# The second self attention's values: copied by ScalarE, with their bias added by a one-row product

## What is computed

```python
def _L1_attn_ref(x, W, b):
    ...
    qkv = jnp.einsum('btc,oc->bto', x, W) + b
    q, k, v = jnp.split(qkv, 3, axis=-1)
    ...
    att = jnp.einsum('bhtd,bhsd->bhts', q, k) / math.sqrt(D)
    att = jnp.where(causal, att, -jnp.inf)
    att = jax.nn.softmax(att, axis=-1)
    y = jnp.einsum('bhts,bhsd->bhtd', att, v)
    return y.transpose(0, 2, 1, 3).reshape(B, T, C)

x = x + _L1_attn_ref(_layernorm(x, axis=-1), L1_attn_W, L1_attn_b)
x = x + _L1_ffn_ref(_layernorm(x, axis=-1), ...)
```

## Time and profile before

| | |
|---|---|
| median of the runs | 1271.08 us |
| the profiled execution, its own time | 1269.69 us |
| its span, first to last instruction | 1267.7 us |
| TensorE busy | 1192.1 us, 94% |
| VectorE busy | 811.6 us, 64% |
| ScalarE busy | 642.3 us, 51% |
| GpSimd busy | 558.4 us, 44% |
| mean granted TensorE clock | 0.995 of full |

### The profile page before, as it was taken

The page is one execution under the profiler, slowest core; times in us unless marked ns, Lnnn a source line. Parts: engine busy times, 40 slices in busy tenths (PEclk is TensorE's granted clock), DMA queues, the critical chain, the costliest instruction groups (busy, mean ns, idle before and its releaser), DMA issues.

```text
span 1267.7 us, 30321 instructions
## 1 busy us (share of the span) xinstructions
PE 1192.1 (94%) x9828; PEld 943.1 (74%) x9828; DVE 811.6 (64%) x1773; ACT 642.3 (51%) x1394; POOL 558.4 (44%) x833
## 2 busy tenths in 40 slices
PE   6899999989998878988999999999999999999998
PEld 5677777767775546877776888888888888888886
DVE  4688888867776887658999784444444544444444
ACT  5766666644444887545556434433334334334342
POOL 2244444567775444458886323233232233232332
PEclk9999999999998999999999999999999999999999
DMA  8100000000000000200000234333333433333331
GB/s 284 59 25 17 17 17 8 1 2 2 0 0 19 15 1 26 75 26 2 0 0 1 76 104 133 104 104 111 116 109 110 133 116 105 109 105 116 114 105 63
DMA packets 34041, 80.13 MB, mean 63 GB/s; under 512 B 4416, under 2 KB 12096, under 8 KB 33984
## 3 DMA queue, kind: packets, MB, share of 16 engines
q1 hardware_dynamic: 32800, 78.09, 18.6%
q10 hardware_dynamic: 1184, 1.31, 0.3%
HBM read 77.03 MB, written 2.36 MB: 63 GB/s over the span
## 4 chain that ended last, share of the span: by engine, by line
PE 78%; DVE 8%; issue 5%; POOL 4%; ACT 4%; DMA 0%; DVEq 0%; POOLq 0%; ACTq 0%; SPq 0%
PE ps L2434 10%; PE ps L2435 10%; PE ps L2433 10%; PE ps L2516 5%; PE ps L2515 5%; PE ps L2517 5%; PE ps L444 4%; PE ps L1095 3%; PE ps L459 3%; PE ps L432 3%; PE ps L1086 2%; PE ps L1074 2%; PE ps L1065 2%; PE ps L1102 2%; POOL Sm L1406 2%
## 5 line engine op out<-in xcount | busy, mean ns | idle before, releaser
L2802 POOL TENSOR_TENSOR sw<-sg,wb 128x512 f32<-128x512 f32 x136 | 176.4, 1297 | 386.7 <-ACT sg L2626 352.8
L2705 DVE TENSOR_TENSOR a<-sw,ps 128x512 f32<-128x512 f32 x136 | 93.5, 687 | 224.7 <-POOL sw L2802 224.4
L2631 ACT ACTIVATE ah<-a 128x512 fp32r<-128x512 f32 x136 | 86.0, 632 | 290.8 <-DVE a L2705 268.5
L2433 PE MATMUL ps<-Hh,wh 128*128 128x512 f32 x544 | 215.8, 397 | 0.2 <-DVE a L2705 0.2
L2434 PE MATMUL ps<-Hl,wh 128*128 128x512 f32 x544 | 214.8, 395 | 0.0
L2435 PE MATMUL ps<-Hh,wl 128*128 128x512 f32 x544 | 214.7, 395 | 0.0
L2709 DVE TENSOR_TENSOR al<-a,ah 128x512 fp32r<-128x512 f32 x136 | 95.6, 703 | 62.5 <-ACT ah L2631 59.3
L760 ACT ACTIVATE Pr<-ps,mx 128x256 f32<-128x256 f32 x256 | 104.0, 479 | 60.9 <-DVE mx L629 56.3
L2433 PEld LDWEIGHTS ps<-Hh,wh 128*128 128x128 f32 x544 | 102.1, 188 | 25.5 <-issue 1.3
L2435 PEld LDWEIGHTS ps<-Hh,wl 128*128 128x128 f32 x544 | 102.0, 188 | 25.0
L2434 PEld LDWEIGHTS ps<-Hl,wh 128*128 128x128 f32 x544 | 102.2, 188 | 23.7
(11 more groups left out here) (238 smaller groups left out, 2488.0 us busy)
## 6 DMA issues: line engine op xcount, KB each, us to landing
wb<-token_weights SPq DMA_DIRECT2D x64, 512.0 KB, 3.6
raw<-in_ew SPq DMA_DIRECT2D x66, 384.0 KB, 3.0
cT<-in_ctxT SPq DMA_DIRECT2D x16, 256.0 KB, 2.6
cx<-in_ctxT SPq DMA_DIRECT2D x15, 256.0 KB, 2.6
X<-in_x SPq DMA_DIRECT2D x1, 1536.0 KB, 7.3
wqkv<-in_wqkv SPq DMA_DIRECT2D x2, 768.0 KB, 5.3
raw3g<-in_wg SPq DMA_DIRECT2D x1, 1024.0 KB, 5.0
raw3u<-in_wu SPq DMA_DIRECT2D x1, 1024.0 KB, 7.1
```

Source lines behind the costliest of these rows:

```text
L2433: eng.matmul(ps[:, bank, :], wh[:, u, w], HhT[:, c, cols], start=(c == 0), stop=False)
L2705: eng.tensor_tensor(a[:, tt, :], sw[:, tt, :], ps[:, UB[tt], :], ALU.mult).then_inc(m_a, 1)
L2802: eng.tensor_tensor(sw[:, tt, :], sg[:, tt, :], wb[:, u, tt * UT:(tt + 1) * UT], ALU.mult).then_inc(m_sw, 1)
```

## The change

In layer 5 alone, the bias is added on TensorE, by a third product into the same accumulation: a column of one row of 128 ones against the one row of 256 biases. The four copies on VectorE become four plain copies on ScalarE, in two halves: two after the copy of hT, two after the exponentials of the second half. Layer 2 keeps the old form.

```diff
             for c in range(2):
                 ins = eng.matmul(ps[:, FV, 0:DIM], hT[:, u, c, :], w[:, c, 2 * DIM:3 * DIM],
-                                 start=(c == 0), stop=(c == 1))
+                                 start=(c == 0), stop=(c == 1 and proj))
+            if not proj:
+                ins = eng.matmul(ps[:, FV, 0:DIM], g["ones"][0:1, :], bv[0:1, :], start=False, stop=True)
             ins.then_inc(a_v, 1)
...
# vector, body
-            if front:
+            if front and proj:
                 v_out(i + 1, v)
...
# vector, first
-            v_out(0, 0)
+            if proj:
+                v_out(0, 0)
...
# scalar
+        def v_out(i, u, half):
+            if half == 0:
+                eng.wait_ge(a_v, given(a_v) + i + 1)
+                eng.wait_ge(a_pv, given(a_pv) + 2 * (i - 1))
+            b = half
+            for e in range(2):
+                eng.activation(V[SEQ * e:SEQ * (e + 1), u, :, b, HD * e:HD * (e + 1)],
+                               ps[SEQ * b:SEQ * (b + 1), FV, 0:DIM].rearrange("p (n e d) -> p n e d", e=2, d=HD)[:, :, e, :],
+                               ACT.Copy).then_inc(a_ve, 1)
...
# scalar, body
             if further(i):
                 ln_act(eng, L, i + 2, u, FH)
+            if front and not proj:
+                v_out(i + 1, v, 0)
             if not proj:
                 g["route"]["turned"](eng, i - 3, v)
             if mid:
                 exps(i, 1)
+            if front and not proj:
+                v_out(i + 1, v, 1)
...
# scalar, first
             ln_act(eng, L, 1, 1, FH)
+            if not proj:
+                v_out(0, 0, 0)
+                v_out(0, 0, 1)
```

## The result

The changed kernel takes 1277.7 us in the median of 4 runs (1276.86 to 1279.19), against 1271.03 us (1270.46 to 1272.88) for the kernel before: 1.0054 times as long, with a 95% interval of 1.0035 to 1.0073. That is 6.7 us slower, outside the forecast range of 1268.6 to 1275.0. The profiled execution took 1276.92 us, with a span of 1275.0 us against 1267.7.

A forecast was written before the change was run, and what follows sets the result against it. TensorE, busy 94% of the span, was taken to set the pace once VectorE was relieved. The terms summed to +1.1 us: 1270.8 profiled, 1272.2 for the median, range 1268.6 to 1275.0.

The forecast's parts named there:

- What bounds the stage: Layer loop: TensorE's own need 7.57 (even) and 7.75 us (odd); VectorE's lateness makes the even body wait for the exponentials.
- rival 1: On TensorE, the one-row product costs next to nothing and only VectorE's relief counts: -3.0 us, 1268.1; chance 0.15.
- the price of the third product: On TensorE, between the values and the first half's transposes in each body: 0.43 us, bounds nothing and 0.54.
- beginning: First values' product, in an unbroken row of TensorE's work ahead of the first scores: +0.43 us; body 0's second: 0.
- bodies 1 to 3: 567.19 to 590.35 us: these bodies already wait at their ends, so the product fills the waits: 0.
- body 4: Even body in the stage: 7.92 us becomes 8.00, +0.08.
- bodies 5 to 12: Four pairs of an odd and an even body: 64.39 us becomes 64.72, +0.33.
- body 13: Odd body in the stage: 7.84 us becomes 8.18, +0.34.
- body 14: Even body near the stage's end: 8.08 us becomes 8.00, -0.08.
- ScalarE's copies: Four copies of 64 x 128 per body, step 0.20 us; the two ahead of the exponentials just fit under TensorE's work.
- rival 2: ScalarE ends last at the second half's exponentials, through two copies ahead of them: +2.7, +3.8 in all, 1274.9; chance 0.13.

The follow-up runs named there:

- full height: The changed kernel with its third product contracting 128 rows of ones against the bias / 128; 1.0015 against the kernel before, 1.9 us over it.
- full height with early and late copies: The late one: the changed kernel with a 128-row third product and all four ScalarE copies behind the second half's exponentials; 1.0003 against the kernel before.
- early copies against late ones beside the one-row product: Late: the changed kernel with all four ScalarE copies behind the second half's exponentials, none ahead of the router's; 1.0043 against the kernel before. Early: the changed kernel.

## Why the prediction was wrong, point by point

**What bounds the stage: right.** VectorE's relief takes the even body from 8.35 to 7.70 us when nothing else is added, and the kernel gains 2.3 us; I had 7.75 and 3.0 for that case (rival 1, the product for nothing). With the product, TensorE's queue sets the pace.

**The step that failed is the price of the third product.** I put "0.43, half of the two, as the nearest row has the same columns and the same accumulation", with 0.54 as the upper bound. It is 0.72 up to the transposes' first record and 0.77 with what the transposes lose. The bound rested on products of full height only. The sum lacked the two changes of height, 128 to 1 and back, across which the weight load is not taken ahead; together they cost 0.34 us per body. The trace before had two signs of it that I passed over. The first load of each values' group, behind the scores of 64 rows, stood idle for 0.38 us, and the row called that "issue". And the 0.54 of the earlier trace rows belongs to a product whose load was not ahead either, since it had waited for UT: its first record has the same step of 0.32 us (555.49 to 555.81). The rule that I cited from the Trainium skill ("TensorE: Matmul & The Clock Gate", "Why this matters for your kernels"), that one product with few rows lasts as long as a full one, agrees for 1 row against 64: 1.69 and 1.68 us. Against full height in this place it does not: 1.40. The measurement decides.

**By the terms of the sum** (from the earlier trace rows and the rows above):

| | forecast | measured |
|---|---|---|
| beginning | +0.43 | 567.87 - 567.19 = +0.68 |
| bodies 1 to 3 | 0 | 24.51 - 23.16 = +1.35 |
| body 4 | +0.08 | 8.50 - 7.92 = +0.58 |
| bodies 5 to 12 | +0.33 | 68.14 - 64.39 = +3.75 |
| body 13 | +0.34 | 8.59 - 7.84 = +0.75 |
| body 14 | -0.08 | 8.29 - 8.08 = +0.21 |
| together | +1.1 | +7.3 |

Of the 6.2 us missing, the changes of height are 5.0 (spans of the changed kernel and of full height, 1275.0 and 1270.0; 4.4 of it in the 13 bodies), and the copies' place is about the rest (1.4 us in the 13 bodies, full height with early and late copies).

**ScalarE's copies: the step was mis-sized, the mechanism right.** I took 0.20 us, within 0.16 and 0.31; it is 0.29. The rows of one copy last 0.27 us, so nothing of one overlaps the next, against the earlier trace rows and against the Trainium skill ("ScalarE: Activation LUTs", "What ACT_TABLE_LOAD costs"), whose 0.2 us for the step supposes an overlap of 93 ns. With it the copies no longer just fit: 2.61 + 0.58 = 3.19 us, where I had 3.01 and TensorE needs 3.04 in an even body and 3.23 in an odd one. By the sum of rival 2 that is 0.15 us in each even body and nothing in the odd ones; measured in the loop, early copies against late ones beside the one-row product, it is 0.18 to 0.21 and 0 to 0.11. Rival 2 thus had the place and the way of adding right.

**That bodies 1 to 3 would absorb the product** held but for 0.3 us for a product of 0.43 (full height: 23.48 us, +0.32), not for 0.72 with early copies (24.51).

**Settled and open.** That the change of height costs, and that neither the number of rows nor a product of few rows by itself does, is shown. Why the load waits there is not; nor why the 64-partition copies do not overlap. Neither was tried further.

## What to carry to other kernels

A product's price depends on its neighbours: before adding a matmul with a small contraction to a stream of full-height ones, think of padding it to full height (here ones against the bias / 128), or of putting the bias elsewhere. In a software pipeline with three engines near full, relief of one is worth only what the others let through (here 0.65 us in an even body and 0.02 in an odd one), so an edit may spend no more than that on the others. Where no projection follows the attention, as here, the value bias needs no matmul at all: it can be added to the residual, in the gap where the vector engine waits.

## What the runs showed of the hardware

- A product of 128 x 256 in 32-bit floats costs a step of 0.43 us with 128 contracted rows between others of 128, and 0.72 with 1 or 64 rows in the same place (0.77 up to the row behind the transposes).
- Where the height changed (64 to 128, 128 to 1, 1 to 128), the weight load stood idle for 0.33 to 0.39 us, which the row calls "issue". The last record in front of the change had a step of 0.31 us, and the first record of a 128 x 256 product behind it 0.32, where a record of such a product has 0.216 in an unbroken row of full-height products.
- Copies of 64 x 128 from PSUM on ScalarE step by 0.29 us at a duration of 0.27.
- GpSimd's subtraction of 128 x 512 took 1.15 us with VectorE's sum of 128 x 256 on SBUF (0.42 us) at its beginning, and 1.04 us in the same kernel without the sum.
